# A decode-style layer stack on one core: the prologue in another order, six key tiles from split parts, sums of squares on ScalarE, and the loops written out

## What is computed

```python
# layer 0: attention over a window of 256 keys in a paged cache (H=8 heads, G=4 key heads, HD=64)
q, k, v = x @ Wq.T, x @ Wk.T, x @ Wv.T
q, k = rope(rms(q, q_norm_scale), pos), rope(rms(k, k_norm_scale), pos)
# the new keys and values are written into the paged cache through block_tables, then
p = softmax(where(allowed, (q @ k_all.T) * 256 ** -0.5, -inf))
x = x + (p @ v_all) @ Wo.T
# layer 1: out[b] = weights[subjects[b]].T @ x[b]   in blocks of 64
# layer 2: x @ W_base.T + (x @ Wt.T @ A.T @ B_w.T @ Wp.T) * scaling, by adapter
# layer 3: x @ W.T + (x @ A.T @ Bm.T) * scalings, by adapter
```

## Time and profile before

| what | us |
|---|---|
| median of 3 runs | 460.89 (460.22 to 461.15) |
| the profiled execution, its own time | 459.73 |
| its span, first to last instruction | 457.9 |
| PE busy | 435.5 (95%) |
| DVE busy | 311.1 (68%) |
| ACT busy | 248.6 (54%) |
| POOL busy | 237.0 (52%) |
| first matmul | 7.2 |
| first transposes of a window (end of the prologue proper) | 97.61 |
| first projection (tile 1 opens) | 130.37 |

### The profile page before, as it was taken

One profiled execution on the slowest core, in us unless ns is written; L12 is line 12 of the kernel. 1 busy time (PEld: TensorE's weight loads), 2 busy tenths in 40 slices (PEclk: granted clock), 3 DMA queues, 4 the chain that ended last, 5 costly groups with the idle time before them and its releaser, 6 DMA issues.

```text
span 457.9 us, 11053 instructions
## 1 busy us (share of the span) xinstructions
PE 435.5 (95%) x3007; PEld 307.7 (67%) x3007; DVE 311.1 (68%) x898; ACT 248.6 (54%) x650; POOL 237.0 (52%) x251
## 2 busy tenths in 40 slices
PE   3999899989699999999999999999999999999995
PEld 1445357456377778777778777777778777877773
DVE  3799998434767676775777676757677776767441
ACT  0524333234447575756665665757575756666651
POOL 1375558675845556473737556555647484451000
PEclk9999999999999999999999999999999999999999
DMA  7546796545837374655556473837365655532122
GB/s 210 170 143 216 210 381 239 167 138 131 236 103 193 77 188 108 160 135 137 137 133 180 84 203 63 211 79 188 85 173 120 162 156 114 161 57 75 25 67 64
DMA packets 75592, 67.29 MB, mean 147 GB/s; under 512 B 50870, under 2 KB 51254, under 8 KB 75539
## 3 DMA queue, kind: packets, MB, share of 16 engines
q1 hardware_dynamic: 60208, 37.97, 30.7%
q0 software_dynamic: 14400, 28.05, 23.1%
q10 hardware_dynamic: 930, 0.72, 0.6%
HBM read 72.49 MB, written 10.22 MB: 181 GB/s over the span
## 4 chain that ended last, share of the span: by engine, by line
PE 81%; DVE 9%; issue 4%; DMA 3%; ACT 2%; POOL 1%; DVEq 0%; SPq 0%; POOLq 0%; ACTq 0%
PE gb L1119 12%; PE ob L1298 10%; PE sbk L1274 10%; PE tb L1287 9%; PE gb L1342 7%; PE gb L1124 6%; PE tb L1260 5%; PE gb L1147 4%; PE gb L1321 3%; PE gb L1347 3%; PE gb L1352 3%; DVE kvo L906 2%; PE gb L1160 2%; PE ob L1332 2%; PE ob L1214 2%
## 5 line engine op out<-in xcount | busy, mean ns | idle before, releaser
L998 DVE CUSTOM_DVE_ANT_0 wide<-sbk,mask 128x336 f32<-128x336 f32 x128 | 60.0, 504 | 62.6 <-PE sbk L1274 46.3
L721 ACT ACTIVATE wide<-wide,negmax 128x336 f32<-128x336 f32 x128 | 72.4, 568 | 25.8 <-DVE negmax L998 18.9
L727 ACT ACTIVATE pt_s<-tb 112x384 f32<-112x384 f32 x128 | 55.7, 488 | 47.5 <-PE tb L1287 44.9
L541 POOL DMA_INDIRECT windows_more<-newkv,idx_b x48 | 48.5, 1011 | 61.9 <-issue 22.6
L541 POOL DMA_INDIRECT windows<-newkv,idx_b x48 | 48.6, 1012 | 47.2 <-issue 20.4
L1287 PEld LDWEIGHTS tb<-cst_late,wide 128*112 128x112 f32 x384 | 44.2, 133 | 20.7 <-issue 10.5
L1287 PE MATMUL tb<-cst_late,wide 128*112 128x128 f32 x384 | 52.7, 273 | 4.1 <-DVE wide L1011 3.3
L1147 PE MATMUL gb<-wkv_s,xt_s 128*128 128x512 f32 x120 | 53.4, 596 | 0.0
L1274 PE MATMUL sbk<-kt_s,qt_s 64*128 64x336 f32 x256 | 52.8, 489 | 0.0
L1011 DVE TENSOR_SCALAR wide<-wide,rinv 128x336 f32<-128x336 f32 x128 | 47.5, 413 | 6.8 <-issue 4.6
L1147 PEld LDWEIGHTS gb<-wkv_s,xt_s 128*128 128x128 f32 x120 | 22.2, 190 | 26.2 <-issue 26.1
(11 more groups left out here) (203 smaller groups left out, 956.3 us busy)
## 6 DMA issues: line engine op xcount, KB each, us to landing
xt_s<-xt_dram SPq DMA_DIRECT2D x31, 256.0 KB, 4.1
newkv<-kvo SPq DMA_DIRECT2D x16, 256.0 KB, 3.0
xtok_s<-xtok_dram SPq DMA_DIRECT2D x16, 256.0 KB, 3.9
up_sel<-up_tab SPq DMA_DIRECT2D x128, 32.0 KB
out_dram<-xo SPq DMA_DIRECT2D x16, 256.0 KB, 4.9
down_sel<-down_tab SPq DMA_DIRECT2D x64, 32.0 KB
wkv_s<-wkv_dram SPq DMA_DIRECT2D x4, 256.0 KB, 6.3
stage<-wq_dram SPq DMA_DIRECT2D x4, 256.0 KB, 3.0
```

The source lines that it names most:

```text
L541: nc.gpsimd.indirect_dma_start(kv_s[r][:, c, :], None, newkv, bass.IndirectOffsetOnAxis(ap=idx_b[r][:, (1, 2, 4)[c]:(1, 2, 4)[c] + 1], axi ...
L721: nc.scalar.activation(prob[i][:, g, :], neg_s[:, g, :], ACT.Exp, bias=negmax[:, g:g + 1], scale=-1.0, accum_out=psum_p[i][:, g:g + 1]).th ...
L727: nc.scalar.activation(pt_s[g][:], tb[g % 2][0:KP, 0:CH * 128].rearrange("p (c q) -> p c q", c=CH), ACT.Copy).then_inc(S["pt_ev"], 1)
L998: V.tensor_tensor_reduce(out=neg_s[:, g, :], in0=sbk[g % 2][:, 0:WK], in1=mask[(t.part(u) + k) % 2][:], scale=-1.0 / 16, scalar=3.0e38, op ...
```

## The change

It reorders the prologue and rewrites the loops; the tiles' own work is the same.

- TensorE multiplies a zeroed qrot four times before the first key tile.
- VectorE makes the angles first and the block index of the gathers after them. All five `same` compares and the queries' angle tables are VectorE's; the latter stand behind the key tiles.
- ScalarE squares each key head by itself, 4 instructions of 128x64, and lets each add up its squares (accum_out); VectorE's sum goes.
- Key tiles 10 to 15 use high and low parts of wkv (kept in m23_s, which is free until the folds) and of xt_s (new buffers xk_s): twelve matmuls on parts in place of four f32 ones.
- The queries and both narrow products stand behind all key tiles, the queries between fold 0 and fold 1, their transposes behind fold 1. GpSimd's identity additions stand behind the last key root.
- The staging ring has five buffers; the last three parts of wo load behind the last store of newkv.
- `Fori` becomes `for` on all five engines.

```diff
             def key_square(n):
-                after(act, S["k_ss"], n - 1)
                 act.wait_ge(S["k_copied"], n + 1)
-                nc.scalar.activation(nr["k"]["sq"][n % 2][:], kvo[n % 4][:, 0:256].rearrange("p (g d) -> p g d", g=G),
-                                     ACT.Square).then_inc(S["k_sq"], 1)
+                for g in range(G):
+                    last = nc.scalar.activation(nr["k"]["sq"][n % 2][:, g, :], kvo[n % 4][:, 64 * g:64 * g + 64], ACT.Square,
+                                                accum_out=nr["k"]["ss"][:, G * n + g:G * n + g + 1])
+                last.then_inc(S["k_sq"], 1)
...
             for n in range(2, TILES):
                 key_copy(n)
+                if n >= SPLIT_A - 2 and n + 2 < TILES:
+                    xk_high(n + 2)
                 key_square(n)
...
+            def wkv_low(c):
+                dve.wait_ge(S["wkv_hi"], c + 1)
+                V.tensor_tensor(m23_s[1][:, c], wkv_s[:, c], m23_s[0][:, c].bitcast(f32), ALU.subtract).then_inc(S["wkv_lo"], 1)
+
+            def xk_low(n):
+                hi, lo = xk_s[n % 2]
+                dve.wait_ge(S["xk_hi"], n - SPLIT_A + 1)
+                V.tensor_tensor(lo[:], xt_s[n % 4][:], hi[:].bitcast(f32), ALU.subtract).then_inc(S["xk_lo"], 1)
...
+            for n in range(SPLIT_A - 1, TILES):
+                if n + 3 < TILES:
+                    xk_low(n + 3)
+                key_tile(n)
...
             def key_tile(n):
 
                 r = n % 4
-                pe.wait_ge(l_xt[r], 16 * (n // 4) + 16)
                 after(pe, S["k_copied"], n - 1)
-                for c in range(C):
-                    last = mm(gb[n % 2][:], xt_s[r][:, c, :], wkv_s[:, c, :], start=(c == 0), stop=(c == C - 1))
+                if n < SPLIT_A:
+                    pe.wait_ge(l_xt[r], 16 * (n // 4) + 16)
+                    for c in range(C):
+                        last = mm(gb[n % 2][:], xt_s[r][:, c, :], wkv_s[:, c, :], start=(c == 0), stop=(c == C - 1))
+                else:
+                    hi, lo = xk_s[n % 2]
+                    pe.wait_ge(S["xk_hi"], n - SPLIT_A + 1)
+                    pe.wait_ge(S["wkv_lo"], C)
+                    for c in range(C):
+                        for b in range(2):
+                            mm(gb[n % 2][:], hi[:, c, :], m23_s[b][:, c, :], start=(c == 0 and b == 0), stop=False)
+                    pe.wait_ge(S["xk_lo"], n - SPLIT_A + 1)
+                    for c in range(C):
+                        last = mm(gb[n % 2][:], lo[:, c, :], m23_s[0][:, c, :], start=False, stop=(c == C - 1))
                 last.then_inc(S["ka_mm"], 1)
...
+            pe.wait_ge(S["blank"], 1)
+            for i in range(4):
+                mm(sbk[0][:], qrot[:, 0:128], qrot[:], start=True, stop=True)
             pe.wait_ge(l_xt[0], 16)
...
-            with pe.Fori(0, 3) as j:
+            for j in range(3):
                 for c in range(1, 5):
                     tile(Tile(j, c), False, False)
```

More of the change, by code:

```diff
@@ L182, in build @@
         single_rows = prepared(len(SINGLE_Q) * 2 * NB).rearrange("p (q k b) -> p q k b", k=2, b=NB)
+        none = prepared(DEPTH * NB).rearrange("p (q b) -> p q b", b=NB)
+        assert _w[0] <= 2 * CH * 512
+        third, fourth = (windows[:, CH * 512 * i:CH * 512 * (i + 1)] for i in (2, 3))
+        sinx, nsinx, cosx = (fourth[:, 512 * i:512 * (i + 1)].rearrange("p (n d) -> p n d", n=TILES) for i in range(3))
+        b2_s = third[:, 1024:1024 + C * 64].rearrange("p (c r) -> p c r", c=C)
         scl2, scl3 = sb("scl2", [128, 1]), sb("scl3", [128, 1])
@@ L243, in build @@
         xt_s += [early(f"xt_s{i}", [128, C, 128]) for i in range(1, 4)]
-        stage = [early(f"stage{i}", [128, 512]) for i in range(STAGES)]
+        stage = [early(f"stage{i}", [128, 512]) for i in range(STAGES - 2)] + [third[:, 512 * i:512 * (i + 1)] for i in range(2)]
         w1_s = early("w1_s", [64, 8, 64])
@@ L276, in build @@
         a2_s = early("a2_s", [128, C, 64])
-        b2_s = early("b2_s", [128, C, 64])
+        xk_s = [[early(f"xk_{w}{i}", [128, C, 128], f32r) for w in ("hi", "lo")] for i in range(2)]
         early_ctx.close()
@@ L395, in _ @@
             store_kv(TILES - 1)
+            for i in range(STAGES, len(splits)):
+                sp.wait_ge(S["split_lo"], i - STAGES + 1)
+                sp.dma_start(stage[i - STAGES][:], splits[i][2]).then_inc(l_stage[i - STAGES], 16)
             sp.wait_ge(S["w1_ident"], 1)
@@ L456, in _ @@
             tile(Tile(0, 2, 2), False, True, True)
-            with sp.Fori(0, TILES // 2 - 3) as j:
+            for j in range(TILES // 2 - 3):
                 for c in (3, 4):
@@ L807, in _ @@
             tile(Tile(0, 0), True, False, True)
-            with act.Fori(0, 3) as j:
+            for j in range(3):
                 for c in range(1, 5):
@@ new lines, in _ @@
+            key_tile(5)
+            key_tile(6)
+            xk_low(SPLIT_A)
+            key_tile(7)
+            xk_low(SPLIT_A + 1)
+            index_rows()
+            key_tile(8)
+            for n in range(SPLIT_A - 1, TILES):
+                if n + 3 < TILES:
+                    xk_low(n + 3)
+                key_tile(n)
+            split_xq(1, xq_first)
+            for i in range(C):
+                split_low(i)
+            for n in range(4):
+                last = angle_table(V, "q", n)
@@ L964, in _ @@
+            last.then_inc(S["qtab_ready"], 1)
+            split_low(4)
+            m23_low(0, tb[0])
             dve.wait_ge(S["qtab_ready"], 1)
             query_tile(Tile(0, 0), 0, None, None, None, sbk[0])
[L966 to L969 removed]
+            split_low(5)
+            m23_low(1, tb[1])
+            split_low(6)
+            split_low(7)
             link(V.tensor_scalar(start[:], k0f[:], -16.0, con("wpos"), ALU.mult, ALU.add))
@@ L1092, in _ @@
             tile(t0, True, False, True)
-            with dve.Fori(0, 3) as j:
+            for j in range(3):
                 for c in range(1, 5):
@@ L1168, in _ @@
             key_tile(1)
+            for n in range(2, 5):
+                key_tile(n)
             HW = BLOCKS * NB // 2
@@ L1181, in _ @@
             last.then_inc(S["sel_mm"], 1)
-            for n in range(2, 6):
+            for n in range(5, 8):
                 key_tile(n)
@@ L1201, in _ @@
             last.then_inc(S["win_mm"], 1)
-            key_tile(7)
-            key_tile(8)
-            lay_index()
             for n in range(9, 12):
                 key_tile(n)
-            pe.wait_ge(S["split_lo"], C)
-            queries(1, sbk[0])
+            lay_index()
+            for n in range(12, TILES):
+                key_tile(n)
             def narrow(bank, width, lhs, rhs, ks=range(C)):
@@ L1237, in _ @@
                       lambda c: w3_s[:, c, :]).then_inc(S["m23_mm"], 1)
+            pe.wait_ge(S["l_wt"], 16 * (C + 1))
+            narrow(ob[0], 64, lambda c, k: wt_s[:, c, 128 * k:128 * k + 128], lambda c: a2_s[:, c, :]).then_inc(S["down2_mm"], 1)
+            pe.wait_ge(S["l_wpt"], 16 * (C + 1))
+            narrow(ob[1], 64, lambda c, k: wpt_s[:, c, 128 * k:128 * k + 128], lambda c: b2_s[:, c, :]).then_inc(S["up2t_mm"], 1)
+            pe.wait_ge(S["wb_ident"], 1)
+            pe.wait_ge(S["w3_ident"], 1)
+            pe.wait_ge(S["idx_ready"], 1)
+            fold(0)
+            pe.wait_ge(S["split_lo"], C)
+            queries(1, sbk[0])
+            fold(1)
+            queries_t(1, sbk[1])
+            fold(2)
+            fold(3)
             def carried(e):
```

269 lines of the change are left out of this document (124 added, 145 removed).

## The result

The changed kernel takes 457.51 us (median of 20 runs, 455.26 to 459.62), the kernel before 461.25 (20 runs, 458.83 to 467.63): a ratio of 0.9918, 95% interval 0.9898 to 0.9938. It is faster, by 0.8%: 3.7 us and not the 8.9 of the forecast, and its 457.5 lies outside the range of 447.5 to 456.5. The profiled execution took 458.0 us with a span of 456.2.

The account below looks back on a forecast made before the run. TensorE was taken to bound the prologue and the tiles behind it. Prologue 2.1 + 3.7 + 1.6 + 2.0 - 2.4 = 7.0 us and loops 1.9 gave 8.9: median 460.89 to 452.0, range 447.5 to 456.5.

Parts of the forecast that it names:

- The warm-up: Before the first key tile: four dummy f32 matmuls raise TensorE's clock, 2.1 us gained; bounds 2.1 gained to 0.9 lost.
- The split tiles: Key tiles 10 to 15 on high and low parts: 2.87 us each against 3.5, 3.7 us off TensorE.
- The key phase: TensorE's sixteen key tiles in the prologue, forecast to end at 64.0 us instead of 82, without a wait.
- The waits of 1.60 and 2.02: TensorE's waits for wq's last low part and the first window gathered from newkv; both were to go.
- The transposes: Query transposes behind fold 1, forecast to wait 1.1 us for the rotated queries, between 0 and 2.
- ScalarE's squares: Four short sums of squares per key tile on ScalarE, forecast at 1.2 us a tile, hidden behind TensorE.
- rival A: Key phase: ScalarE or the ring of four key buffers becomes the bound, squares 1.6 us a tile; 455.5 us, chance 0.18.
- The loops: Loops written out: 2.9 us removed at turn openings, 1.0 given back by eight tiles at 0.12; net 1.9.
- rival D: Written-out tiles: code fetch costs each of twelve 1.6 us, slower than before; 470.2 us, chance 0.05.
- the wait of fold 0: Behind the narrow products: TensorE waits 1.3 us for GpSimd's identity additions, forecast to end at 72.3; between 0 and 3.
- the last root: GpSimd's root of the last key tile, ahead of the additions: not before 67.1 us, some 68.5 with two gathers.
- 3 if VectorE's last tiles run two us late: Upper bound in us on fold 0's wait for GpSimd's additions, where the forecast took 1.3.

Follow-up runs that it names:

- id_dve: Changed kernel with both identity additions on VectorE, W_base's ahead of the last key tile and W3's behind it: 452.6 us against 457.3.
- the third group: Runs on one chip: kernel before 462.2 us, unaltered changed kernel 457.30, without warm-up 459.42, both additions on VectorE 452.6, these plus dummy matmuls 450.97.
- best: Changed kernel with both identity additions on VectorE and dummy matmuls in tile 0 and the last stage: 450.97 us, 0.9761 of the kernel before.
- id_mid: Changed kernel with GpSimd's first two gathers of old rows moved behind both identity additions: 466.9 us, no unaltered kernel beside it.
- id_mid_q: As id_mid, with the queries' root also ahead of the first gathers of new rows on GpSimd: 465.24 us, no unaltered kernel beside it.
- squares_dve: Changed kernel with keys squared in one ScalarE instruction per tile and summed on VectorE, as before the change: 465.24 us against 461.54.

## Why the prediction was too low

**What held.** The warm-up: 1.7 us in the traces, 2.1 when taken away (forecast 2.1). The split tiles: 2.7 us apart (2.87), 3.3 when taken away (3.7), though not by the path of the sum. The key phase ended at 63.46 (64.0). The waits of 1.60 and 2.02 went. The transposes waited 1.03 (1.1). ScalarE's squares cost about 1.0 a tile (1.2), so rival A did not come. The loops gave 1.8 (1.9), and code fetch (rival D) cost no more than the 0.12 a tile.

**What failed first: the wait of fold 0, 3.50 us where the sum has 1.3.** TensorE was on time (70.7, forecast 71.0); the additions ended at 74.1 and not at 72.3. The step that was wrong is the last root. I let it follow the last key tile by copy, squares and mean, at 66, and gave 1.4 for the gathers. But VectorE, which runs its tiles in order, stood still 0.94 us for the 15th root and reached the last tile's mean only at 67.9; then the gather of single rows held GpSimd until 68.9. The last root ended at 70.2, 1.7 us behind the estimate, and the additions took 3.95. That the last key tile did not set the last root here is what the kernel without the split shows: its key phase ended 3.5 us later, and its additions started only 0.3 later. And with the additions moved to VectorE (id_dve) the wait was 0.81. The bound that I had named, "3 if VectorE's last tiles run two us late", is what came; I took 1.3, nearer the other end, because I added up VectorE's busy time and left out its waits for roots.

**What failed second: a term that was missing, the clock.** All prices in the sum were read at 2.4 GHz, from an execution whose granted clock never fell. The change made TensorE's longest wait behind the first matmul 3.50 us instead of 2.02, and in all four traces of the unaltered changed kernel the clock fell at it. I had priced a wait as its own length. The prologue's miss of 4.1 us (2.9 gained, 7.0 forecast) is then 1.9 of later start, 1.9 of slow fold and some 0.3 of the first query matmul, which is still slow. The profiled execution lost 1.4 us more in tile 0 and 1.4 in the last stage, 4.7 with the 1.9 of the fold. These two falls stand behind waits that the kernel before has as well (1.99; 0.58, 0.79 and 0.76), at full clock in its first trace and with falls in its second, so no run shows that they come of the change: they belong to the pair of executions.

The whole: 8.9 forecast, less 1.9 of later start, less 4.7 of clock, less 0.3, is 2.0, near the 1.7 between the two profiled executions. The medians differ by 3.7, since the kernel before, too, loses to the clock in many of its runs while its profiled execution was one without a fall; the changed kernel's was a usual one. That pair of executions thus flatters the kernel before, and the forecast took its prices from it. For the medians the sum is 8.9 - 1.9 - 1.9 - 0.3 = 4.8 against 3.7: some 1.1 us stay unexplained. That the change costs about one fall more than before agrees with the third group, where the median run of the kernel before has a mean clock of 0.996 and that of the changed kernel 0.989.

**What stays open.** Which waits are followed by a fall. In the unfilled changed kernel (four traces) the one of 3.2 to 3.5 us always was. Of the variants, those of 0.81 and 1.05 at fold 0 in id_dve and best were not, and those between went both ways: 1.67 in best and 1.73 in id_mid without, 2.25 in id_mid_q and 2.40 without the split with, 1.99 in tile 0 without before and with after. Nor is it settled why the groups, each on another chip, differ by up to 16 us for the kernel before, nor what squares_dve lost.

## What to carry over

Price a new wait of TensorE at more than its length: look whether the granted clock falls behind it, and if so either move the producer or give TensorE dummy matmuls. When an engine's end is estimated, follow the loop of hand-overs (root, rotation, next root) and not the sum of its busy time. Take the base of a forecast from an execution whose clock is that of the usual run.

## What the runs showed of the hardware

- Dummy matmuls whose result nobody reads shortened the kernel by 4.0 and 5.1 us, with TensorE busier than without (446.9 us against 445.0, and 444.3 against 441.9).
- GpSimd and VectorE slowed each other where both read SBUF: a VectorE step of 0.43 us took 2.74 beside the additions on GpSimd, and the eight additions 6.2 us instead of 4.0 where VectorE had more instructions beside them (four of them on VectorE took 0.89). The Trainium skill (SBUF — State Buffer, SBUF: two separate sides) calls the port pair that the two share an exclusive lock, which whoever starts first has for a whole instruction while the other blocks. The trace agrees that VectorE stands still; but it does so for longer than the one instruction: its step starts 0.05 us behind the first addition (0.44 us) and ends only during the seventh.
- Four ScalarE sums of 128x64 start 0.24 us apart, although each takes 0.24 and an accumulator read of 0.19 follows it: the read overlaps the next one.
- The kernel before differed by up to 16 us between chips (461.25 to 477.16), and the changed one by at most 5.5: the ratio of the two moved from 0.9918 to 0.9735.
